# A graph network on one core: VectorE's order of work at the start of a group of edges

## The reference, cut to what matters

```
h = relu(layernorm(x))
xp = (h @ W).reshape(n, 4, 32)                      # 4 heads
e = leaky_relu(a_s[src] + a_d[dst])                 # one number per edge and head
m = segment_max(e, dst); e = exp(e - m[dst])
out = segment_sum(e * xp[src], dst) / segment_sum(e, dst)
x = x + relu(out + bias)                            # layer 0
h = relu(layernorm(x))
agg = segment_sum(edge_attr @ We + be, dst)
c = concat(h, agg); z = c + segment_sum(c[src], dst)
x = x + relu(z @ W1 + b1) @ W2 + b2                 # layer 1
```

## Time and profile before

| | us |
|---|---|
| runs before (median, lowest, highest) | 2648.06, 2647.75, 2650.3 |
| profiled execution, its own time | 2646.39 |
| its span, first to last instruction | 2644.6 |
| the loop over the groups, from DVE's first copy of logits to its last | 126.7 to 2178.8 |
| POOL busy in the span | 1518.4 |
| DVE busy in the span | 1794.5 |
| PE busy in the span | 1961.1 |
| mean granted clock of TensorE | 0.814 |

### The profile page before, as it was taken

The page is one execution under the profiler, slowest core; times in us unless marked ns, Lnnn a source line. Parts: engine busy times, 40 slices in busy tenths (PEclk is TensorE's granted clock), DMA queues, the critical chain, the costliest instruction groups (busy, mean ns, idle before and its releaser), DMA issues.

```text
span 2644.6 us, 63796 instructions
## 1 busy us (share of the span) xinstructions
PE 1961.1 (74%) x16211; PEld 1625.0 (61%) x16211; DVE 1794.5 (68%) x6198; ACT 1084.4 (41%) x2295; POOL 1518.4 (57%) x1626
## 2 busy tenths in 40 slices
PE   4277777776777767767777777767776776999998
PEld 3266556655565556655565556655665554888887
DVE  7578777887778777878787777877787775111111
ACT  3044544554454545454454545544445443000000
POOL 5377777776776777777776777767776760000000
PEclk9587778777887778777877787778877887999999
DMA  9966667666776767666776776767766666666663
GB/s 177 156 198 204 213 224 230 208 214 211 232 226 188 224 225 221 214 203 227 230 218 195 221 231 211 214 207 232 229 204 201 229 207 230 216 216 217 217 216 135
DMA packets 276907, 560.29 MB, mean 212 GB/s; under 512 B 113395, under 2 KB 211139, under 8 KB 248081
## 3 DMA queue, kind: packets, MB, share of 16 engines
q1 hardware_dynamic: 226763, 444.37, 49.3%
q0 software_dynamic: 50112, 115.56, 19.4%
HBM read 382.53 MB, written 177.22 MB: 212 GB/s over the span
## 4 chain that ended last, share of the span: by engine, by line
PE 48%; DMA 14%; issue 11%; DVE 10%; POOL 8%; ACT 4%; SPq 3%; ACTq 1%; DVEq 1%; POOLq 0%
PE pv L1135 14%; DMA big<-table,idx 12%; PE pv L1250 10%; POOL big L812 8%; PE pv L1196 7%; PE pt L1250 5%; PE pt L1125 4%; ACT xsb L848 3%; PE pm L1163 2%; PE pa L1125 2%; PE pa L1179 2%; ACT big L848 1%; DVE state L1538 1%; PE pm L1144 1%; ACTq L901 1%
## 5 line engine op out<-in xcount | busy, mean ns | idle before, releaser
L812 POOL DMA_INDIRECT big<-table,idx x1566 | 1485.1, 948 | 628.2 <-issue 424.4
L848 ACT ACTIVATE xsb<-pt 128x343 f32 x1042 | 476.4, 457 | 758.9 <-PE pt L1127 444.5
L1135 PE MATMUL pv<-big 128*128 128x128 f32 x3132 | 486.7, 319 | 6.7 <-ACT big L848 6.7
L1135 PEld LDWEIGHTS pv<-big 128*128 128x128 f32 x3132 | 451.6, 229 | 38.3 <-issue 19.9
L1125 PE MATMUL pt<-tabb 128*128 128x343 bf16 x1042 | 389.8, 374 | 50.9 <-ACT xsb L848 46.8
L1196 PE MATMUL pv<-big 128*128 128x133 f32 x3132 | 390.9, 279 | 0.0
L1196 PEld LDWEIGHTS pv<-big 128*128 128x128 f32 x3132 | 367.9, 190 | 4.4
L1479 DVE TENSOR_TENSOR tabb<-pc,keyp 128x2064 bf16<-128x2064 bf16 x261 | 319.1, 1222 | 0.0
L1250 PE MATMUL pv<-big,xsb 128*128 128x384 bf16 (+1 forms) x1617 | 278.9, 329 | 18.5 <-DVE big L1781 18.5
L848 ACT ACTIVATE xsb<-pa 128x343 f32 x521 | 238.4, 458 | 90.3 <-ACT xsb L848 66.3
L1250 PEld LDWEIGHTS pv<-big,xsb 128*128 128x128 bf16 (+1 forms) x1617 | 230.2, 147 | 52.1 <-issue 21.0
(11 more groups left out here) (291 smaller groups left out, 2970.4 us busy)
## 6 DMA issues: line engine op xcount, KB each, us to landing
adj<-xsb SPq DMA_DIRECT2D x87, 1568.0 KB
big<-in_edge_attr_dram SPq DMA_DIRECT2D x87, 1152.0 KB
xsb<-adj SPq DMA_DIRECT2D x33, 1568.0 KB, 6.1
selb<-rel SPq DMA_DIRECT2D x87, 576.0 KB
tabb<-adj SPq DMA_DIRECT2D x16, 1568.0 KB, 6.2
big<-table,idx POOLq DMA_INDIRECT x1566
state<-sums SPq DMA_DIRECT2D x87, 130.5 KB
sums<-state SPq DMA_DIRECT2D x87, 130.5 KB
```

Source lines behind the costliest of these rows:

```text
L812: pool.indirect_dma_start(out=V[b][:, j, 0:rows], out_offset=None, in_=table, in_offset=bass.IndirectOffsetOnAxis(ap=index[b][:, j:j + 1], ...
L848: return nc.scalar.activation(out_, in_, func, **kw).then_inc(s(name), 1)
L1135: ins = nc.tensor.matmul(sumA[b], SEL[b][:, j, :], AT[b][:, j, :], start=(j == 0), stop=(j == J - 1))
```

## The change

Only DVE's `item` changes. Three things that stood behind the wait for the gathered rows now stand ahead of it: `select`, the copy of the mask `last` into the 13th column of `peaks`, and `rescale_state` of the group before. Nothing is added or taken away, and no semaphore changes its meaning; the waits inside the moved functions (`mg_b` and `selc_b` of the group before in `select`; `s_load` and `fold_b` of the group before in `rescale_state`) move with them.

```
@@ -1636,6 +1636,11 @@
                 v.tensor_scalar(cont4[:, :, 1:J], isl[:, bass.DynSlice(g, 1), 0:J - 1].to_broadcast([128, H, J - 1]),
                                 -BIG, None, ALU.mult).then_inc(s("cont_b"), 1)
+                select(n, b, extra_group)
+                last = isl[:, bass.DynSlice(g, 1), :].rearrange("p a (j c) -> p (a j) c", c=1)
+                v.tensor_copy(peaks[:, :, NK * H:NK * H + 1], last).then_inc(s("pkl_b"), 1)
+                if m is not None:
+                    rescale_state(m, 1 - b)
                 dve.wait_ge(s(f"gat{b}"), it * 16 * J + 16 * J)
                 v.tensor_copy(logit[:, :, :], V[b][:, :, C:C + H].rearrange("p j h -> p h j"))\
                     .then_inc(s("log_b"), 1)
@@ -1645,9 +1650,6 @@
                                      logit[:, :, :].rearrange(flat), -BIG, ALU.add, ALU.max)\
                     .then_inc(s("pre1_b"), 1)
-                select(n, b, extra_group)
-                if m is not None:
-                    rescale_state(m, 1 - b)
                 after(dve, s("thru_c"), n)
                 after(dve, s("tailT_b"), n)
@@ -1667,8 +1669,6 @@
                 between(finish_residual)
-                last = isl[:, bass.DynSlice(g, 1), :].rearrange("p a (j c) -> p (a j) c", c=1)
-                v.tensor_copy(peaks[:, :, NK * H:NK * H + 1], last).then_inc(s("pkl_b"), 1)
                 after(dve, s("pre2_b"), n)
```

## The result

| | before | after |
|---|---|---|
| runs on the same chip, median (lowest, highest; number), us | 2648.06 (2645.07, 2650.3; 5) | 2630.15 (2626.42, 2638.78; 5) |
| ratio of the times, 95% interval | | 0.9942 (0.9929 to 0.9954) |
| profiled execution, its span, us | 2646.39, 2644.6 | 2626.42, 2624.5 |
| loop, first to last copy of the logits, us | 126.7 to 2178.8 | 130.1 to 2158.9 |
| DVE's wait for the gathered rows, us | 350.9 | 233.7 |

The change makes the kernel 0.58% faster, 18 us between the medians, where 36 had been forecast. The runs of the changed kernel also lie wider apart (12 us) than those of before (5 us).

What follows compares the result with a forecast made beforehand. DVE's wait for gathered rows and POOL's waits for DVE's chain were taken to bound the loop. Halfway between 47 us (turn kept) and 25 us (only long waits) gave 36 us: 2610, as a median 2612, range 2586 to 2645 us.

Steps and rivals of the forecast that it cites:

- the landing of the rows: Time from POOL's last transfer ending to rows arriving: 5.09 us for long after long, 2.84 us for a short wait.
- Long and short waits, set by the store: In the loop, an adjacency store issued well ahead of POOL's end makes a long wait: 5.77 us landing against 2.84.
- 1.0 us in a long-wait group: After a long wait, `tails` and the chain behind it start 1.0 us earlier, and POOL follows fully.
- 0.1 us in a short-wait group: After a short wait PE's transpose holds `tails`, so only the mask gains: 0.1 us, between 0 and 0.2.
- Cover, and the wait for `state`: DVE's idle time before the rows hides the moved 1.84 us, about 1.0 us remaining; the `state` load wait costs 0.
- A mixture, half of the long-wait groups followed by a long one: Loop forecast: half the long-wait groups followed by short, half by long waits; 36 us faster, chance 0.34.
- Such a group lasts 23.57 us, one that a short wait follows 21.40: Copy-to-copy interval after a long wait: 24.57 less 1.0 us if a long wait follows, 21.4 if a short one.
- the sign that I named: Telltale on DVE: the multiplications of `state` show no idle time before them.
- The edge itself: Lead of the store over POOL's end at which a wait turns from short to long: between 0.10 and 0.46 us.
- Rival 3: All loop waits long, each as long as the longest, 24.27 us a group: 35 us slower, 2681; chance 0.10.
- that the store's place would hardly matter: DMA engines alternate gather and store packets, so issue order hardly counts and the gain would be 47 us.

Runs made afterwards that it cites:

- e1: Kernel before, with SP issuing a group's adjacency store only when the next group's gathered rows have landed: 2551.8 us, ratio 0.9628.
- e9: Kernel before, with the adjacency store issued one place earlier, ahead of the store of the projected rows: 2791.19 us, ratio 1.0541.
- e10: Changed kernel, with the adjacency store issued one place earlier, ahead of the store of the projected rows: 2710.53 us, ratio 1.0231.
- e2: Changed kernel, with SP issuing a group's adjacency store only when the next group's gathered rows have landed: 2545.4 us, ratio 0.9602.
- e3: Kernel before, with only `select` moved ahead of the wait for rows: 2639.34 us, ratio 0.9961.
- e6: Changed kernel, with three unread 128-column products added on PE ahead of the products for `mg`: 2640.36 us, ratio 0.9971.
- e4: Kernel before, with only `rescale_state` moved ahead of the wait for rows: 2648.13 us, ratio 0.9995.
- e7: Changed kernel, with the adjacency store held until the next rows landed and three unread products on PE ahead of `mg`: 2543.39 us, ratio 0.9601.
- e11: Kernel before, with six unread products added on PE ahead of the transpose of `pre1`: 2652.01 us, ratio 1.0012.

## Why the prediction was right or wrong

The sign, the range and the mechanism held; the gain was half of what I forecast, 18 us for 36. The step that failed is the landing of the rows, a term of both sizes of a group after a long wait. By its own steps:

- *Long and short waits, set by the store.* Right. e1 and e9 move the store alone, and the kernel goes from 2552 to 2791 us.
- *1.0 us in a long-wait group.* Right: `tails` 1.17 to 1.21 us after the copy, POOL's end at 18.5 us, and 0.94 us a group between e9 and e10, where the kinds are the same in both.
- *0.1 us in a short-wait group.* Right as far as can be told: 0.07 us a group between e1 and e2, within the noise. The wait that is late next is the one that was named, `tails` for PE's transpose.
- *Cover, and the wait for `state`.* Right in the cost, which I took as 0: the copy waits for the rows in all 86 groups, so nothing ahead of it held it up. Wrong in the sign that I named: there are 36 waits before the multiplications, 30.0 us, where I had said none. POOL's waits for `cback_b` fell to 50.6 us, where 40 had been said, and DVE's wait for rows to 233.7 where 190 had been: both go with the landings, of which more are long than in a loop that keeps its turn.
- *A mixture, half of the long-wait groups followed by a long one.* Met, 30 of 56, but by luck: the half was a guess between two cases, derived from nothing, and 38 of 61 in e3 and 49 of 67 in e6 show that the share moves. Nor is the sum for it right. If half of the long-wait groups are followed by a long one, a third of all groups are of that kind, so by my own sizes it is 2/3 x 47 + 1/3 x 25 = 40 us and not 36; and the pair's mean of 23.82 us in place of the loop's 23.86 hid another 3.
- *Such a group lasts 23.57 us, one that a short wait follows 21.40.* Here the forecast failed, in size. They last 23.97 and 21.78 us. POOL's part was right (18.5 us); the landings were not, 5.48 us in place of 5.09 and 3.23 in place of 2.84. With my sizes for each kind (21.40, 23.57, 25.13, and 23.3 put in for the two short pairs, which the prediction has no size for) the 85 counted intervals come to 1988.6 us; they took 2008.8. Of these 20 us, 30 x 0.40 = 12.0 are the long-after-long ones, 26 x 0.38 = 9.9 the long-then-short ones, and the rest -1.7. With my sizes the loop would have been 43.5 us shorter than before; it was 23.3 us shorter. The landings took the other half.

Why the landings were mis-sized: I took 5.09 from the only long-after-long case in the trace, with the store 0.46 us ahead. 595 landings of seven kernels (before, after, e3, e4, e6, e9, e10) show that this was the edge, not the plateau:

| store ahead of POOL's end by, us | landings | mean landing, us |
|---|---|---|
| over 0.5 behind | 30 | 3.39 |
| 0 to 0.5 behind | 88 | 3.10 |
| 0 to 0.2 | 24 | 2.96 |
| 0.2 to 0.4 | 15 | 3.76 |
| 0.4 to 0.6 | 17 | 5.09 |
| 0.6 to 0.8 | 33 | 5.47 |
| 0.8 to 1.0 | 64 | 5.69 |
| 1.0 to 1.5 | 203 | 5.77 |
| 1.5 to 3.0 | 115 | 5.73 |
| over 3.0 | 6 | 4.65 |

The edge itself was read rightly, between 0.10 and 0.46 us. But a shift that lets the store come sooner leads beyond it, to 5.5 us and more. With 5.5 in place of 5.09 a long-after-long group is 18.5 + 5.5 = 24.0 us, and a loop of nothing else 86 x 0.14 = 12 us slower than before, not 25 faster. The short landing of 2.84 us was that of one pair; in the trace of before such landings are 3.01 us in the mean. In the changed kernel they are 3.23, with the store 0.30 us behind POOL's end in place of 0.04; what adds the last 0.2 us is not shown. A third of the groups at each of 21.78, 23.97 and my 25.13 us is 23.63 on average, 86 x 0.23 = 20 us faster than before, near the 23.3 of the profiled loop and the 18 between the medians.

Rival 3, slower by long waits everywhere, had the right point to decide from (a mean landing of 5.36 us), and its price of 24.27 us a group lies between what such groups took in the changed kernel (23.97) and in e10 (24.64). The landings of the changed kernel's long-after-long groups are past it, 5.48; it was not met since only 30 groups were of this kind. e10 is what it looks like in full: 2.3% slower.

The page "DMA: Bandwidth & Descriptors" of the Trainium skill, section "Queues, rings and completion order", has each DMA engine take its queues in turn, packet by packet. What I drew from it, that the store's place would hardly matter, is not borne out: a landing goes from 3.0 to 5.8 us as the store moves by about a microsecond. Nor do the packets of the two pass each other in the long wait of the earlier trace rows. From 1029.20 to 1031.90, and then to 1033.80, the queue of SP's transfers (q1) and that of the gather (q0) moved (packets, MB, share of the 16 engines):

```profile
q1 hardware_dynamic: 89, 1.12, 97.9%
q0 software_dynamic: 1, 0.00, 0.0%
...
q0 software_dynamic: 137, 0.34, 57.0%
q1 hardware_dynamic: 27, 0.14, 18.2%
```

The rows whose last transfer POOL had issued by 1027.98 are there at 1033.75 only; for 2.7 us of that the gather's queue moves one packet, while the store's moves 1.12 MB. Why the engines did not take turns is not shown.

What stays open: what makes PE's attribute sums come early in half of the groups after a long wait. The clock is the candidate (above), and the two kernels that were to test it in the kernel before did not move it where it counts. The spread of 12 us between runs of the changed kernel would fit a varying share of the kinds: a long-after-long group lasts 0.57 us more than the 23.40 of a pair in turn ((21.78 + 25.03)/2), so 21 groups make 12 us. Only its fastest run has a trace, and this is argued, not shown.

## What to carry to other kernels

Before costing an earlier start of a chain, ask which bulk transfer is issued behind it and lands among the small ones that somebody waits for; a gain of 1 us in every second group was here half given back, since in many groups the store came some 0.9 us sooner against the gather's end. Size such a collision from the plateau of many landings, not from the one that looks like the new case. And the better change was beside this one: a wait that holds the 1568 KB store until the rows have landed makes the kernel before 3.7% faster and the changed one 4.0% (2545.4 us; with e7's idle products 2543.39, within its spread), after which POOL's 18 transfers of 1.25 us are the bound.

## What the runs showed of the hardware

- When the adjacency store is issued 0.6 to 3 us ahead of the end of the last indirect transfer, the gathered rows land 5.5 to 5.8 us after that end in the mean, in place of some 3.1 when it is issued up to 0.5 us behind. The DMA share is 1.00 to 1.05 then. Where the store is held back they take 1.80 us (e1). Nearly the whole step lies between 0.2 and 0.6 us of lead.
- In one such wait the gather's queue moved a single packet in 2.7 us, beside 1.12 MB of the store's queue (before, 1029.20 to 1031.90).
- One store of SP, moved past one other store, costs 5.4% (e9); one wait ahead of it gives 3.7% (e1).
- A mean granted clock of 0.86 in the loop in place of 0.79 (e11, for products that nobody reads) bought nothing, 1.0012 (1.0003 to 1.0022).
